# First pair of x: transposed through DRAM and VectorE's blocks instead of on TensorE

## The reference

```
Q = layernorm(x) @ Wq.T + bq ;  K = ctx @ Wk.T + bk
x1 = x + softmax(Q @ K.T / sqrt(1024)) @ ctx
w  = scales[g_idx] * (where(nibble(qweight) > 0, 1, -1) - (nibble(qzeros) + 1))
out = x1 + layernorm(x1) @ w + bias
```

## Time and profile before

| | us |
|---|---|
| median of 3 runs | 547.48 (547.1 to 548.16) |
| profiled execution, whole | 547.35 |
| its span, first to last instruction | 545.6 |

### The profile page before, as it was taken

How to read it: one execution, slowest core, us unless ns; L and a number is a source line. 1 busy time by engine, 2 the same in 40 slices (tenths; PEclk the granted TensorE clock), 3 DMA queues, 4 the chain that set the end, 5 groups by cost and what they waited for, 6 DMA issues and landing times.

```text
span 545.6 us, 7455 instructions
## 1 busy us (share of the span) xinstructions
PE 539.3 (99%) x2686; PEld 452.0 (83%) x2686; DVE 372.4 (68%) x616; ACT 268.0 (49%) x474; POOL 187.2 (34%) x147
## 2 busy tenths in 40 slices
PE   8999999999999999999999999999999999999997
PEld 7888888887777877778898999998788888888886
DVE  4989775787698774793424555574768779778742
ACT  6983444414767582343437766686563243324210
POOL 1072000010011000000326877777756644753530
PEclk9999999999999999999999999999999999999999
DMA  8942100359688756836384899898346775774311
GB/s 270 314 157 79 38 1 0 123 156 313 195 228 292 204 193 193 262 86 192 126 293 144 298 362 355 321 389 346 144 123 244 220 216 203 230 232 134 98 77 77
DMA packets 56036, 108.14 MB, mean 198 GB/s; under 512 B 12000, under 2 KB 32552, under 8 KB 53824
## 3 DMA queue, kind: packets, MB, share of 16 engines
q1 hardware_dynamic: 49472, 101.38, 54.1%
q10 hardware_dynamic: 6528, 6.29, 5.7%
HBM read 67.74 MB, written 39.85 MB: 197 GB/s over the span
## 4 chain that ended last, share of the span: by engine, by line
PE 86%; DVE 4%; ACT 3%; DMA 3%; issue 1%; POOL 1%; ACTq 0%; SPq 0%; DVEq 0%; POOLq 0%
PE bank L1337 22%; PE bank L1339 22%; PE bank L1338 22%; PE bank L1384 5%; PE bank L1390 5%; PE bank L1387 5%; PE bank L1438 2%; DMA xq<-xn_scratch 1%; ACT yin L868 1%; POOL cn_lo L578 1%; DVE xq L1035 1%; DMA wq_stage<-in_L_xattn_Wq 1%; DVE xT_lo L932 1%; PE bank L1347 1%; ACT cn_hi L627 1%
## 5 line engine op out<-in xcount | busy, mean ns | idle before, releaser
L1337 PE MATMUL bank<-xT_hi,m_hi 128*128 128x512 f32 x256 | 101.0, 395 | 0.0
L1339 PE MATMUL bank<-xT_hi,m_lo 128*128 128x512 f32 x256 | 99.7, 390 | 0.0
L1338 PE MATMUL bank<-xT_lo,m_hi 128*128 128x512 f32 x256 | 99.6, 389 | 0.0
L585 POOL TENSOR_TENSOR tT_lo<-t_pair,tT_hi 128x1024 fp32r<-128x1024 f32 x16 | 38.1, 2398 | 75.4 <-ACT tT_hi L627 75.4
L1289 DVE TENSOR_TENSOR xres<-xres,bank 128x512 f32<-128x512 f32 x56 | 38.3, 683 | 36.1 <-PE bank L1339 36.0
L599 POOL TENSOR_TENSOR l_lo_s<-l_sum_s,l_hi_s 128x512 fp32r<-128x512 f32 x32 | 40.4, 1297 | 56.0 <-DVE l_sum_s L1230 56.0
L824 ACT ACTIVATE t_pair<-bank,ucol 128x512 f32<-128x512 f32 x32 | 22.0, 687 | 74.1 <-PE bank L1339 69.6
L1337 PEld LDWEIGHTS bank<-xT_hi,m_hi 128*128 128x128 f32 x256 | 48.0, 188 | 11.8 <-issue 2.1
L1339 PEld LDWEIGHTS bank<-xT_hi,m_lo 128*128 128x128 f32 x256 | 48.0, 188 | 10.2
L1338 PEld LDWEIGHTS bank<-xT_lo,m_hi 128*128 128x128 f32 x256 | 48.1, 188 | 10.0 <-issue 0.2
L1384 PE MATMUL bank<-wk_hi,wq_hi 128*128 128x512 f32 x128 | 50.5, 394 | 0.2 <-DVE wq_lo L932 0.2
(11 more groups left out here) (158 smaller groups left out, 1244.0 us busy)
## 6 DMA issues: line engine op xcount, KB each, us to landing
xres<-in_x SPq DMA_DIRECT2D x8, 1024.0 KB, 11.9
out<-xres SPq DMA_DIRECT2D x15, 512.0 KB, 5.2
right_scratch<-part_hi SPq DMA_DIRECT2D x28, 256.0 KB, 2.2
cin<-in_ctx SPq DMA_DIRECT2D x7, 1024.0 KB, 6.1
xn_scratch<-xin SPq DMA_DIRECT2D x6, 1024.0 KB, 4.7
xq<-xn_scratch ACTq DMA_DIRECT2D x24, 256.0 KB, 5.4
r_tile<-right_scratch SPq DMA_DIRECT2D x6, 1024.0 KB, 12.2
yn_scratch<-yin SPq DMA_DIRECT2D x6, 1024.0 KB, 4.0
```

Of the source, the lines that this page charges most:

```text
L585: pool.tensor_tensor(tT_lo[b][:, ks, :], t_pair[b // 2][:, b % 2, ks, :], tT_hi[b % 2 if b else 2][:, ks, :].bitcast(F32), ALU.subtract).t ...
L1337: pe.matmul(out_, a_hi, b_hi, start=start, stop=False, skip_group_check=True)
L1338: pe.matmul(out_, a_hi, b_lo, start=False, stop=False, skip_group_check=True)
L1339: return pe.matmul(out_, a_lo, b_hi, start=False, stop=stop, skip_group_check=True)
```

## The change

1. The layer norm of batches 0 and 1 moves from DVE (blocks 4 and 5) to ACT (blocks 3 and 4): `x_stats` stands between the first split and `times_bk`, `x_apply` behind the second split.
2. The 32 transposes on PE are gone.
3. SP, behind its last load of Wq, stores each of the two batches with eight transfers of 128 KB. Source pieces in SBUF are of 32 numbers (128 B), 1024 pieces in a transfer; in DRAM each partition's eight pieces follow one another (1 KB). Then it reads batch 0 back by four transfers of 256 KB (pieces of 1 KB), and batch 1 the same way.
4. DVE transposes batch 0 by blocks in block 6, ahead of `sum_bk(6)` and the second half of Wq block 7, and batch 1 at the head of block 7.
5. All eight `x_hi` of the pair wait for both batches' blocks. All eight `x_lo` stand ahead of `copy_u`.

```
+            for b in range(2):
+                sp.wait_ge(s_xn, QT * (b + 1))
+                for t in range(QT):
+                    pieces = xin[:, b, t, :].rearrange("p (k a i) -> p a k i", k=NB, a=4)
+                    for a in range(4):
+                        sp.dma_start(xn_dram[b, t * P:(t + 1) * P, a * S:(a + 1) * S].rearrange("p (k i) -> p k i", k=NB),
+                                     pieces[:, a, :, :]).then_inc(s_xst0[b], 16)
+            for b in range(2):
+                sp.wait_ge(s_xst0[b], 16 * 4 * QT)
+                rows = xn_dram[b].rearrange("(m j) f -> j m f", j=32)
+                for a in range(4):
+                    sp.dma_start(xq[0][32 * a:32 * a + 32, b * NB:(b + 1) * NB, :], rows[:, :, a * S:(a + 1) * S]
+                                 ).then_inc(s_xq0[b], 16)
...
@@ ACT, blocks of the projection
                 elif 1 < b < NB - 1:
                     wq_split(b + 1, 0)
+                    if b in (3, 4):
+                        x_stats(b - 3)
                     times_bk(b)
                     wq_split(b + 1, 1)
+                if b in (3, 4):
+                    x_apply(b - 3)
                 if b == NB - 1:
-                    for u in range(6):
+                    for u in range(NB):
                         x_hi(0, u)
...
@@ DVE, blocks of the projection
-                if b in (4, 5):
-                    x_stats(b - 4)
-                    x_apply(b - 4)
+                if b >= NB - 2:
+                    x_blocks(b - (NB - 2))
...
                 if b == NB - 1:
-                    for u in range(5):
+                    for u in range(NB):
                         x_lo(0, u)
                     copy_u()
-                    x_lo(0, 5)
...
@@ PE, block 7
-                        for u in {3: (0, 1), 4: (2,), 5: (3, 4), 6: (5,), 7: (6, 7)}.get(c, ()):
-                            x_tr(u)
```

More of the change, by code:

```diff
@@ L159, in xattn_ffn_kernel @@
         xjunk = [at(f"xjunk{t}", 188.25 + 2 * t, [P, D], BF16) for t in range(QT)]
+        xjunk_early = [at(f"xjunk_early{t}", 61.75 + 2 * t, [P, D], BF16) for t in range(QT)]
         cn_hi = at("cn_hi", 178.25, [P, QT, D], F32R)
@@ L680, in _, with x_stats @@
                 times_bq(c)
+            def x_stats(b):
+                if b < 2:
+                    act.wait_ge(s_xl[b], 16)
+                    rows, places = xin[:, b, :, :], xjunk_early
+                    if b == 0:
+                        act.wait_ge(s_uacc, NB - 1)
+                else:
+                    act.wait_ge(s_xraw[b % 2], 16 * (b // 2))
+                    rows, places = raw_rows(b), xjunk
+                    if b == KH:
+                        act.wait_ge(s_placed, 16 * 8)
+                        act.wait_ge(s_xn, QT * KH)
+                for t in range(QT):
+                    act.activation(places[t], rows[:, t, :], ACT.Copy, accum_out=xsum[:, t:t + 1]).then_inc(s_xsum, 1)
+                act.wait_ge(s_xsum, QT * ON_ACT[b])
+                act.activation(nmean, xsum, ACT.Copy, scale=-1.0 / D).then_inc(s_xmean, 1)
+                act.wait_ge(s_xmean, ON_ACT[b])
+                for t in range(QT):
+                    act.activation(places[t], rows[:, t, :], ACT.Square, bias=nmean[:, t:t + 1],
+                                   accum_out=xsquares[:, t:t + 1]).then_inc(s_xsq, 1)
@@ new lines, in x_apply @@
+            def x_apply(b):
+                act.wait_ge(s_rstd, b + 1)
+                if b >= 2:
+                    act.wait_ge(s_xst, 16 * (b - 2))
+                    act.wait_ge(s_dot, b)
+                for t in range(QT):
+                    if b < 2:
+                        out_, in_ = xin[:, b, t, :], xin[:, b, t, :]
+                    else:
+                        out_, in_ = by_quadrant(xin[:, 1, t, :]), raw_rows(b)[:, t, :].rearrange("q (k a i) -> q k a i", k=NB, a=4)
+                    act.activation(out_, in_, ACT.Identity, bias=shift[:, t:t + 1], scale=rstd[:, t:t + 1]).then_inc(s_xn, 1)
@@ L682, in x_hi @@
             def x_hi(p, u):
+                act.wait_ge(s_xT, 2 * p + 2)
                 if p == 0:
-                    act.wait_ge(s_xtr, u + 1)
                     act.wait_ge(s_wqused, NB)
-                    copy(xT_hi[:, u, :], bank[6 + u % 2][:, :]).then_inc(s_xhi, 1)
-                else:
[L688 to L694, removed]
+                elif u < NB - 1:
+                    act.wait_ge(s_xused, (NB - 1) * (p - 1) + u + 1)
+                else:
+                    act.wait_ge(s_t, NB * p)
@@ L696, in _ @@
+                copy(xT_hi[:, u, :].rearrange("p (m j) -> p m j", j=32), xq[p][:, :, 32 * u:32 * u + 32]
+                     ).then_inc(s_xhi, 1)
             for b in range(NB):
@@ L1011, in x_stats @@
             def x_stats(b):
[L1012 to L1017, removed]
+                dve.wait_ge(s_xraw[b % 2], 16 * (b // 2))
+                ln_stats(raw_rows(b))
             def x_apply(b):
@@ L1038, in x_lo @@
                 dve.wait_ge(s_xhi, NB * p + u + 1)
[L1039 to L1043, removed]
+                low(xT_lo[:, u, :].rearrange("p (m j) -> p m j", j=32), xq[p][:, :, 32 * u:32 * u + 32],
+                    xT_hi[:, u, :].rearrange("p (m j) -> p m j", j=32), s_xlo)
             def copy_u():
```

75 lines of the change are left out of this document (24 added, 51 removed).

## The result

The changed kernel took 553.51 us in the median of six runs (551.83 to 553.76), against 547.82 us of the kernel before in six runs: a ratio of 1.0097, 95% interval 1.0087 to 1.0107. That is 5.7 us slower, where 2.9 us slower was forecast. The profiled execution took 553.39 us, its span is 6.0 us longer than before.

A forecast was written before the change was run, and what follows sets the result against it. PE's instruction list was taken as the bound; the removed 3.5 us return as stalls of about 1.7 and 4.5 us, so the t stage begins at 103.95 instead of 101.05, 2.9 us later: 550.4 us, range 545.6 to 559.

The forecast's parts named there:

- landing of the reload: Batch 0's reload behind all 16 stores: 5.4 us from the last issue to landing, landed at 85.2 us.
- What bounds it: Up to 101 us PE's instruction list bounds the time; a shift of the t stage's start shifts the end.
- ACT in blocks 3 and 4: Layer norm there: statistics 4.75 us, `times_bk(4)` to 64.15; second half of Wq just in time, then 0.3 us late.
- The price of a store: SP's 16 stores of 1024 pieces of 128 B: 0.91 us each, first two 0.55, 13.7 us in all.
- From S to the t stage: DVE's queued work, copies of u and PE's row sum, from batch 0's block transpose to the t stage: 18.75 us.
- S: Start of DVE's block transpose of batch 0, forecast at 85.2 us after DVE stands 6.4 us.
- PE's two waits: PE stalls about 1.7 us at slice 4 of block 7 and 4.5 us before the row sum.
- Rival 1: Stores limited by issuing alone, 0.55 us each: a gain of 1.7 us, 545.7; chance 0.19.
- Rival 2: Stores in between, 0.77 us each, 12.3 us: +1.5 us, 548.9; chance 0.12.
- Rival 3: Writes of 128 B to DRAM dearer than reads: 558.3 at one and a half times, +18, 565.5 at twice; chance 0.16.
- Rival 4: As forecast, but TensorE's clock falls in the 4.5 us PE stands, costing 1.7 us: +4.6, 552.1; chance 0.10.

The follow-up runs named there:

- e2: The changed kernel with DVE's block transposes of both batches behind `sum_bk(7)`, at the head of block 7: 550.12 us, 1.0049 against the kernel before.

## Why the prediction was wrong

The direction was right and so was the chain of waits, but the loss was twice the size forecast. The step that failed is the landing of the reload. Step by step:

- **What bounds it: right.** A shift of the start of the t stage is a shift of the end, as long as it goes later: 5.7 us there, 5.7 in the medians. (Towards earlier this stops at DVE's list, as the copies-early kernels showed.) In the profiled executions the last eviction of t is another 0.4 us late. A gather at 247.37 waits 0.6 us for DVE where it waited 0.2, and a store to `right_scratch` landed in 4.71 us instead of 3.35. In the traces of the six kernels above that keep the small stores and the late copies of u (e2, the two with PE kept busy, reload 1 held back, reload 0 ahead, `times_bk` first) that gather waits 0.2 us, so the 0.4 us belongs to this one execution.
- **ACT in blocks 3 and 4: right.** Statistics took 4.73 us (45.87 to 50.60) for 4.75, and `times_bk(4)` started at 61.94 and ended at 64.38 for 64.15. Behind this, PE came to the end of block 5 at 72.96 instead of 72.08; 0.45 of that was there at the start of block 3 (45.33 for 44.88 in the earlier trace rows), ahead of any edit.

```profile
45.33 0.63 ACT L647 ACTIVATE wq_hi<-wq_stage 128x512 fp32r<-128x512 f32 x1 [3.53 <-PE bank L1402]
...
50.60 2.44 ACT L675 ACTIVATE wq_bk<-wq_stage,bcols 128x128 f32<-128x128 f32 x8
...
61.94 2.44 ACT L675 ACTIVATE wq_bk<-wq_stage,bcols 128x128 f32<-128x128 f32 x8
```

- **The price of a store: right in the mean, in part by luck.** 14.39 / 16 = 0.90 us each, for 0.91 by the earlier trace rows, and 14.5 us to the first reload for 13.7. But no steady 0.90 lies behind it. From the fifth to the thirteenth the stores follow one another by 0.74 us ((75.12 - 69.17) / 8), and two took far longer:

```profile
66.70 1.80 SPq L452
...
76.80 1.97 SPq L452
```

  What made these two long is open.
- **The landing of the reload: the step that failed**, "4.9 us to landing in the median, 6.1 at most; I take 5.4 ... Landed: ... 85.2 us". DVE started at 88.08, 2.88 us later, after 8.3 us of standing where 5 to 8 were forecast. Of the 2.88, 0.3 is the later start of the stores, 0.8 the stores, 0.35 the spacing of the four issues (1.69 for 1.35), and 1.45 the landing: 6.84 us from the last issue. The 4.9 of the earlier trace rows was the median of single transfers of another tile; the eight reloads here (DMA to landing, min/median/max) had

```profile
L460 SPq DMA_DIRECT2D xq<-xn_scratch x8: 302/452/631, 79.5 to 83.5; - x8
DMA to landing us min/median/max: 4.5/6.7/9.2
```

  and DVE waits for the last of four. The trace of before showed such a reload, in the chain of waits of the t stage, with a 1 MB store still moving when it began (375 GB/s from 206 to 208 us) and nothing of the change in it:

```profile
209.02 7.07 DMA xq<-xn_scratch
```

  With 7.0 in place of 5.4 the forecast would have been +4.5.

  What the term lacked is what else was in the queue. The two reloads with nothing beside them (batch 1's with reload 0 ahead and with reload 1 held back) had 5.6 and 5.3 us for the slowest of the four, and the first of them spaced its issues by 1.35 us in all: the forecast's 5.4 and 1.35 nearly to the number. With the last stores ahead it was 6.4, with the other reload behind as well 6.8, with small stores behind 6.6, with a 1 MB store still moving and the other reload behind 7.0. My 5.4 held 0.5 us for the stores, on top of the median of 4.9, and nothing for the reload of batch 1. From first issue to DVE's start that is 7.0 us alone and 8.0 to 8.55 with neighbours; 9.5 in the kernel with `times_bk` first (84.07 - 74.53) is open. Each of these is one execution, so how much of it the stores and how much the second reload cost is an estimate from these rows; that other work in the queue goes with a landing 0.8 us or more later is what all of them show.
- **From S to the t stage: right.** 106.74 - 88.08 = 18.66 us for 18.75.
- **PE's two waits: right in kind, wrong in size.** 3.6 and 2.7 us for 1.7 and 4.5. The later S lengthens the first; the second is shorter since PE came to it later and did the work between them partly at the lower clock.
- **Rival 1 (issue alone, 545.7): not what happened.** Its "against" misread a row, though: with cq's share of 0.80 the DMA engines were not "nearly full", since the stores ran at a share of 1.58 (row below). And one store of 4 KB pieces gave its figure, 546.12: a gain of 1.2 us was all that this order of DVE left of the 3.5.
- **Rival 2 (0.77 us a store, 548.9): wrong in the mean** of 0.90, though most stores did follow one another by about that.
- **Rival 3 (dear writes of 128 B): refuted.** The stores moved 174 GB/s at a DMA share of 1.58, cq's reads of the same piece 143 GB/s at 0.80:

```profile
70.00:78.00 8.00, 8.00 (x37) 6.64 (x36) 3.89 (x4) 2.59 (x7) 0.00 (x0) 1.00 1.58 174
```

  The share is higher, the time per piece is not. The Trainium skill (DMA: Bandwidth & Descriptors, Specifications) says that below 512 B the DMA engines read, modify and write. No row here shows whether they did; the runs show that these writes, eight pieces in a row in DRAM, cost no more than reads of 128 B, while the same 2 MB in 4 KB pieces occupied SP for 2.52 us. Writes that do not follow one another were not tried.
- **Rival 4 (the clock falls): half right.** The clock did fall in the changed kernel, 0.57 in the window 92 to 96 us (0.51 from 94 to 96), about its lower level, 1.2 GHz. But it fell behind the first wait, where the second hid it, and its price at the end was nothing. The place I had feared, the row sum, kept its clock behind a wait of 2.7 us; behind 3.5, 4.3 and 7.3 us there it lost it, for 1.6 to 2.1 us. The forecast's price of 1.7 us agrees with that by luck: it came from the slow transposes at the start, where the granted clock reads 1.00, so that the clock was their cause is not shown. The window of the changed kernel at its row sum:

```profile
104.00:106.00 2.00, 1.22 (x3) 0.68 (x4) 1.85 (x5) 0.18 (x2) 0.00 (x0) 1.00 1.03 424
```

  The Trainium skill (TensorE: Matmul & The Clock Gate, Part 1) says that PE has to be busy again before it gets 2.4 GHz, and the trace agrees with that: the matmuls directly behind the wait ran at the lower level (0.51 from 94 to 96 us), and from 96 us on the granted clock was 1.00.

## What to carry to other kernels

A set of transfers is as long as from its first issue to the landing of its last member: take it from a wait on such a set in the trace, not from a median of single transfers, and look what else was in the queue at that wait (here 7.0 us alone, 8.0 to 8.55 with neighbours). Before a long job is given to an engine that feeds the critical one, list what stands behind the waiting instruction, and put early what the critical engine asks for first (here the copies of u). Time taken off the critical engine counts only up to the slack of the next engine's list, here 0.7 us of DVE at the first gather, and if the critical engine must stand anyway, the place matters, since the clock that it loses is paid only where no later wait hides it.

## What the runs showed of the hardware

- Stores from SBUF to DRAM in 128 B pieces: 0.90 us in the mean for 1024 pieces with the queue full (0.74 most of the time, two of 1.80 and 1.97), 3.3 to 4.6 us to landing, no dearer than loads of the same size (0.91).
- Four transfers of 256 KB in 1 KB pieces, read from DRAM into 32 partitions each: 7.0 us from the first issue until the waiting engine starts with nothing else in the queue, 8.0 to 8.55 with stores or a second set beside them, 9.5 once. The slowest of the four landed in 5.3 and 5.6 us alone and in 6.4 to 7.0 with neighbours.
- The granted clock was still 1.00 behind a wait of PE of 2.7 us at the row sum, and 0.57 to 0.61 behind waits of 3.5, 3.6 and 4.3 us (windows of 4 us); behind 7.3 us it was 0.50. In the kernel with reload 1 held back it fell to 0.50 (92 to 94 us) behind a wait of 2.8 us at slice 4 of block 7. Transposes of float32 in the gap kept it at 1.00.
